# Two MoE layers on one core: groups 2 and 3 between the layers in a new order, and the last pages' results summed by TensorE

## What is computed

```
x = x + xattn0(ctx, layernorm(x))                 # 8 heads, masked
x = x + ffn0(layernorm(x))                        # top 2 of 8 experts (704 wide), silu(g)*u, and a shared one
h = rmsnorm(layernorm(x)) @ W_in.T + b_in
x = x + depool(rmsnorm(ctx)) + h                  # a scan over patches, one patch for many tokens
z = layernorm(x)
scores = sigmoid(z @ gate_w.T)                    # 32 experts in 8 groups
top 6 of the best 4 groups, weights normalised, * 2.5
x = x + sum over the 6 of weight * (relu(z @ up_w[e].T)**2 @ down_w[e].T)
      + relu(z @ shared_up.T)**2 @ shared_down.T
```

## Time and profile before

| | us |
|---|---|
| median of 3 runs | 887.16 (883.94 to 887.17) |
| the profiled execution | 888.47 |
| its span, first to last instruction | 886.6 |
| PE busy | 722.6 (82%) |
| DVE busy | 416.7 (47%) |
| ACT busy | 273.0 (31%) |
| POOL busy | 308.5 (35%) |
| layer 1's shared units and the steps of groups 2 and 3 | about 558 to 665 |
| layer 1's routed experts | about 670 to 859 |
| last results read back and summed | 859 to 887 |

### The profile page before, as it was taken

The page is one execution under the profiler, slowest core; times in us unless marked ns, Lnnn a source line. Parts: engine busy times, 40 slices in busy tenths (PEclk is TensorE's granted clock), DMA queues, the critical chain, the costliest instruction groups (busy, mean ns, idle before and its releaser), DMA issues.

```text
span 886.6 us, 14153 instructions
## 1 busy us (share of the span) xinstructions
PE 722.6 (82%) x4526; PEld 631.4 (71%) x4526; DVE 416.7 (47%) x1615; ACT 273.0 (31%) x620; POOL 308.5 (35%) x322
## 2 busy tenths in 40 slices
PE   3868886389999999999899888866776868787865
PEld 2647776289999999999899877533456757676754
DVE  4998664022333243546644742725104444456563
ACT  2636631022111111222223122321123455445540
POOL 1333307600010111100552354172712656556560
PEclk9898859589999999999999998796978899989998
DMA  8999992231776767755866624242646556587866
GB/s 257 396 296 268 257 252 97 102 125 53 231 231 219 218 221 244 246 169 190 304 218 232 217 89 170 92 166 87 217 154 189 177 158 191 164 288 243 285 215 250
DMA packets 93534, 181.22 MB, mean 204 GB/s; under 512 B 9857, under 2 KB 54998, under 8 KB 93182
## 3 DMA queue, kind: packets, MB, share of 16 engines
q1 hardware_dynamic: 78048, 138.67, 50.9%
q0 software_dynamic: 13344, 38.68, 11.6%
q10 hardware_dynamic: 2046, 2.71, 1.0%
HBM read 134.07 MB, written 65.62 MB: 225 GB/s over the span
## 4 chain that ended last, share of the span: by engine, by line
PE 56%; DVE 16%; issue 10%; another core or an unknown queue 6%; DMA 4%; ACT 3%; POOL 3%; SPq 1%; DVEq 0%; POOLq 0%; ACTq 0%
PE PB L618 16%; PE PB L655 11%; PE PB L632 5%; PE PB L825 4%; PE PB L816 4%; PE PB L763 3%; POOL rows_out L1930 3%; PE PB L777 2%; PE PB L804 2%; DMA X<-in_x 2%; PE PB L684 1%; PE PB L600 1%; DMA MEM<-rows_out 1%; DVE WK L1256 1%
## 5 line engine op out<-in xcount | busy, mean ns | idle before, releaser
L618 PE MATMUL PB<-XT,MEM 128*128 128x128 f32 x1584 | 185.9, 276 | 1.1 <-issue 1.1
L618 PEld LDWEIGHTS PB<-XT,MEM 128*128 128x128 f32 x1584 | 181.7, 193 | 1.5 <-issue 1.3
L1882 POOL DMA_INDIRECT sorted_y<-WK x36 | 34.5, 958 | 279.0 <-DVE WK L1470 279.0
L1891 POOL DMA_INDIRECT rows_in<-MEM x96 | 93.5, 974 | 65.1 <-DVE MEM L1674 36.6
L655 PE MATMUL PB<-MEM,WK 128*128 x432 | 99.7, 380 | 3.3 <-DVE MEM L1646 1.9
L825 PE MATMUL PB<-MEM,WK 128*128 x228 | 67.6, 424 | 32.0 <-DVE WK L1823 26.1
L655 PEld LDWEIGHTS PB<-MEM,WK 128*128 128x128 f32 x432 | 79.3, 190 | 13.2 <-issue 3.9
L1930 POOL DMA_INDIRECT rows_out<-WS,MEM x58 | 56.7, 977 | 64.4 <-ACT WS L1045 49.2
L825 PEld LDWEIGHTS PB<-MEM,WK 128*128 128x128 f32 x228 | 42.2, 207 | 41.2 <-issue 36.9
L1930 POOL DMA_INDIRECT rows_out<-MEM x56 | 56.2, 1003 | 40.5 <-ACT MEM L1045 25.7
L939 ACT ACTIVATE XT<-PB 128x256 f32<-128x256 f32 x52 | 19.8, 381 | 162.2 <-PE PB L600 134.2
(11 more groups left out here) (280 smaller groups left out, 1255.4 us busy)
## 6 DMA issues: line engine op xcount, KB each, us to landing
MEM<-in_w SPq DMA_DIRECT2D x36, 896.0 KB
rows_in<-in_consts SPq DMA_DIRECT2D x32, 600.0 KB, 12.2
MEM<-in_w SPq DMA_DIRECT2D x36, 512.0 KB
MEM<-rows_in SPq DMA_DIRECT2D x58, 300.0 KB
MEM<-rows_out SPq DMA_DIRECT2D x16, 768.0 KB, 7.0
MEM<-in_w SPq DMA_DIRECT2D x32, 256.0 KB, 2.8
MEM<-in_w SPq DMA_DIRECT2D x2, 3072.0 KB, 18.9
sorted_x<-MEM SPq DMA_DIRECT2D x1, 5070.0 KB, 39.7
```

The lines of the kernel that those rows point to most:

```text
L618: t = e.matmul(o[:, to:to + P], UPW[m][i % (3 - m)][:, k, c * P:(c + 1) * P], XT[:, n % 2, k, :], start=(k == 0), stop=(k == 1))
L1882: e.indirect_dma_start(out=DY, out_offset=bass.IndirectOffsetOnAxis(ap=DEST[:, i:i + 1], axis=0), in_=YS[:, i % 2, :], in_offset=None).the ...
L1891: e.indirect_dma_start(out=DX1, out_offset=bass.IndirectOffsetOnAxis(ap=SLOT1[:, i, j:j + 1], axis=0), in_=XR[:, i, :], in_offset=None).th ...
```

## The change

**A. The order between the layers.** "t1" of group 2 moves into the middle of the up product of block 34 (`SOON`), "wi" into the same block, "t2" to block 35; "ro" of group 2 now stands before the two late shared tiles' up products. "rank" is split: PE's part and `shares` stand before the last `down`, `slots` right behind it and ahead of group 3's "sum". Group 3's "q1" and "q2" are shared by ACT (two tiles) and DVE (two). Units 0 to 3 stand before group 3's "q1", "ro" of group 3 behind unit 5's `up1`. An item ("u", n), ("d", n) or ("drain", n) is `up1`, `down1` or DVE's add alone.

```diff
+STEP_AT2 = 0, 1, 1, 2, 3, 4
+SOON = {(SUM_AT[2] + 1, 1)}
...
-        ("turn", 1), ("down", -1), ("wi", 2), ("up", 0), ("q2", 2), ("up", 1), ("t2", 2), ("down", 0), ("ro", 2), ("down", 1),
+        ("turn", 1), ("down", -1), ("t2", 2), ("ro", 2), ("up", 0), ("up", 1), ("down", 0), ("rank", 2), ("shares", 2),
```

```diff
+OWN = (TOPK * GB[3] + E1) // 2
...
+def up_bank(s):
+    return 4 + s % (4 if s < OWN - 2 else 2)
...
+            def to_tokens(s, n_pairs):
+                q.wait_ge("by", s)
+                q.wait_ge("hot", s)
+                q.wait_ge("bh", OWN - 3)
+                for b in (2 * s, 2 * s + 1):
+                    last = b == 2 * n_pairs - 1
+                    for i in range(4):
+                        t = e.matmul(PB[:, 6 + i // 2, i % 2 * D:(i % 2 + 1) * D], HOT[b % 4][:, i * P:(i + 1) * P], YO[b % 4],
+                                     start=(b == 2 * OWN and i % 2 == 0), stop=last, skip_group_check=True)
...
+                if OWN <= s - 2 < n_pairs:
+                    to_tokens(s - 2, n_pairs)
...
-                for i in range(8, NT, 2):
-                    o = PB[:, i // 2, 0:D]
...
+            def one_hot(s):
+                for b in (2 * s, 2 * s + 1):
+                    t = e.tensor_scalar(HOT[b % 4], TOKENS, PT6[:, s // 2 % 2, b % 4:b % 4 + 1], None, ALU.is_equal)
...
+                        e.tensor_tensor(X[:, i - 1:i + 1, :], X[:, i - 1:i + 1, :],
+                                        PB[:, 6 + h, :].rearrange("p (t d) -> p t d", t=2), ALU.add).then_inc(
...
+                if 0 <= s - 2 < OWN:
...
+            for i in range(8, NT, 2):
+                y = Y6[place(i)]
+                q.wait_ge(f"l6_{place(i)}", i)
+                e.tensor_tensor(y[:, 0:3 * D], y[:, 0:3 * D], y[:, 3 * D:6 * D], ALU.add).then_inc(*q.mark("set1"))
+                for k in (1, 2):
+                    e.tensor_tensor(y[:, 0:D], y[:, 0:D], y[:, k * D:(k + 1) * D], ALU.add).then_inc(*q.mark("set1"))
+                e.tensor_tensor(X[:, i, :], X[:, i, :], y[:, 0:D], ALU.add).then_inc(*q.mark("sp", i))
...
+                if i in (6, 8, 10, 12):
+                    lo = TRASH + (GB[3] + i // 2 - 3) * P * TOPK
+                    e.dma_start(DY1[lo:lo + P * TOPK, :].rearrange("(p n) d -> p n d", p=P),
+                                ZERO[:, 0:D].unsqueeze(1).broadcast_to([P, TOPK, D])).then_inc(*q.land("zeroed1", i))
...
             def fetch6(i):
+                upto = min(TOPK * GB[GROUP[i] + 1] + E1, 2 * OWN) - 1
...
+            store(6)
+            for i in range(8, NT):
+                fetch6(i)
```

```diff
+ENDS = {s: s - 2 for s in range(2, NPR + 2)}
+ENDS[1] = ENDS.pop(2)
```

More of the change, by code:

```diff
@@ L961, in mid @@
                         q.wait_ge("t1", g - 1, 1)
-                    for i in range(4):
+                    for i in range(4 if g < 3 else 2):
                         t = e.activation(to[:, i, :], X[:, a + i, :], ACT.Identity, bias=R2[:, a + i:a + i + 1],
@@ L1065, in end1 @@
                     step(s, n_pairs)
[L1066 to L1070 removed]
+                for h in range(2):
+                    i = GB[3] + 2 * h
+                    q.wait_ge("total", h)
                     e.dma_start(od[:, i:i + 2, :], X[:, i:i + 2, :]).then_inc(*q.land("out_b", i))
```

218 lines of the change are left out of this document (136 added, 82 removed).

## The result

| | before | changed |
|---|---|---|
| median of 4 runs, us | 887.16 (883.94 to 896.89) | 899.65 (897.6 to 900.65) |
| ratio, 95% interval | | 1.0144 (1.0104 to 1.0184) |
| profiled execution, its span | 888.47, 886.6 | 900.34, 898.5 |
| first page's fetch | 666.89 | 673.87 |
| from there to the end | 219.7 | 224.6 |

What follows compares the result with a forecast made beforehand. It took PE to bound layer 0's blocks, POOL's row bursts to hold PE between the layers, and DMA latency and POOL the end. 888.5 - 12 - 5 = 871.5 profiled, so 870 us; range 850 to 884.

Steps and rivals of the forecast that it cites:

- Step (2): Between the layers: group 2's `shares` and `slots` end at 559.3, so its row burst starts 12.4 us sooner.
- step (1): Between the layers: group 2's picks no longer cost the path, so PE's unit 0 starts 3 to 4 us sooner.
- Step (4): Between the layers: the burst ends 12.4 us sooner, so the first hold ends at about 593, if PE's group 3 work precedes it.
- R2: Rival: between the layers PE is held as long, ro of group 3 after the hold; middle -2, 880 us, 16%.
- Step (3): Between the layers: group 3's sums come 6 us later on DVE, covered by units; priced at nothing, up to 4 us otherwise.
- Step (5): Between the layers: 11.7 us from sigmoid to first row DMA, so the second burst starts at 605 instead of 617.5.
- Step (6): Between the layers: what follows the second hold, four to five units, stays the same.
- The reading of the holds: Between the layers: from some 11 to 15 us into a POOL burst, handovers with PE arrive only when it is over.
- B, the end: Kernel's end: chains of DMA, PE and POOL all give 881 to 882 against 886.6, so -5 us.
- R4: Rival: at the end PE's added products run at its lower clock; +20 there, 895 us, slower, 6%.
- R3: Rival: the end gives nothing because POOL and DVE share ports; 875 us, 10%.
- The rule against B: Kernel's end: a shared-port lock would make POOL's and DVE's sums go in turn, giving 0 instead of -5.

Runs made afterwards that it cites:

- order_only: The kernel before with only the new order between the layers, the end as before: 902.38 us, 1.0072 of the kernel before.
- dve_sums: The changed kernel with POOL's four sums given to DVE, which sums all of tiles 8 to 15: 903.28 us, 1.0071 of the kernel before.
- end_only: The changed kernel with the new order between the layers taken back: 901.82 us, 1.0066 of the kernel before.
- late_memset: The kernel before with one small memset of POOL behind everything: 898.51 us in one execution.
- end_dve: The changed kernel with the old order, DVE summing tiles 8 to 15, and one store behind five fetches: 899.99 us, 1.0052 of the kernel before.
- no_burst2_c: The changed kernel without 23 of group 2's 24 row DMAs, zeros written instead, those rows missing: 885.76 us, 0.9878 of the kernel before.
- before_again: The kernel before, unchanged, profiled once more in a set without long waits: 773.64 us.
- after_again: The changed kernel as it is, run in a set without long waits: 777.86 us, 1.0015 of the kernel before.

## Why the prediction was wrong, point by point

**Step (2), group 2's places at 559.3.** They came at 566.4. `slots` take 5.1 us (561.30 to 566.37), but they stand behind the adds of both late shared tiles (557.47 and 560.97), and those wait for PE's `down`, which came later: DVE's `hidden` (L1503) was held until 556.94. That the row burst of group 1 held it follows from the theory of the bursts and was not tested there. The step took DVE's list as full and the shared results as done at 557.7, though the new order puts the picks ahead of their products. So step (1), unit 0 sooner by 3 to 4 us, became 3.3 later.

**Step (4) is the one that failed.** It said that the hold's end moves with the burst's end, to 593, provided that PE has done t1, wi, t2 and ro of group 3 before the hold. It had not. The burst moved 5.3 us ahead and "wi" 7.3 us back (571.41 before, 578.72 now), so "wi" fell 12 us into the burst instead of at its start, and two late signals that had lain elsewhere now stood one behind the other on the path, with t2 and ro after them. The sigmoid starts at 612.79 instead of 605.80: 7.0 us later, in these two traces the whole of the stage's loss (in the others it starts at 609.22 and 610.80 with the new order and at 603.38, 605.17 and 607.61 with the old). This is R2's place, "ro of group 3 comes after the hold", but R2 priced it at -2 and it cost +7, because the condition of step (4) was named and not checked: by its own numbers PE had to be done with ro by 559.5 + 15 = 574.5, where the kernel before does ro at 589.39 (PE's L704) and the new order puts more in front of it.

**Step (3), group 3's sums later on DVE, priced at nothing, or up to 4 us.** The sums now start at 566.28, behind the places, and q1, t1 and "wi" move back with them. That is how "wi" came into the hold: the price was sought in PE's cover and lay in the hold.

**Step (5), 11.7 us from the sigmoid to the burst,** held exactly: 612.79 to 624.50. Only its start was wrong. **Step (6)**, that what follows is the same, held between these two: from the burst's start to the first page's fetch it is 49.37 us in both (617.52 to 666.89, 624.50 to 673.87). That is partly luck. In the other traces with holes the stretch is 50.2 and 49.8 us with the new order (order_only, dve_sums) but 53.7, 52.5 and 52.5 with the old (end_only, late_memset, end_dve), so there the old order loses in the second burst some 3 us of what it had gained before it.

**The reading of the holds.** The profile of before could only suggest it, and no_burst2_c showed it. What was wrong in it is how a hold runs: it does not end once with the burst, but signals come in batches, the last some 4 us behind the burst. The trace of before has a batch in the middle already (ACT's timeline, then PE's):

```profile
593.08 0.60 ACT L1014 ACTIVATE WK<-PB 128x512 f32<-128x512 f32 x1 [4.96 <-PE PB L763]
...
584.25 3.27 PE L763 MATMUL PB<-MEM 128*128 128x512 f32 x4
```

This relu, the fifth of L1014 in the stage, is that of unit 4, whose `up1` PE ended at 587.52; it starts 5.6 us late, and 21 us into the burst, where the prediction let nothing through from 11 to 15 us on. The sign of "a hole that ends later than 3 us after the burst" came (600.56 against 596.87), and before has it too: its sigmoid starts at 605.80, 3.8 us behind its burst.

**B, the end, -5 forecast, +4.9 measured.** The step that failed is the join of the three chains, "the last of eight is there at 875.5. DVE's sum 2.34": it let one sum stand behind the fetches, while DVE has four to do and stands with all of them behind its last `one_hot`, and so behind PE. No sum of DVE waited for a DMA (its rows above have no bracket); the first began at 878.85, behind the last matrix. PE's chain was forecast to end at 877.9; 7.1 us that pair 51 came later with the middle (848.07 to 855.19) and 2.8 for the one pair at the lower clock make 887.8, and it ended at 887.96: R4's mechanism, met in one pair of five. POOL's chain was 15 us and took 19.1 (870.60 to 889.67), DVE's four tiles were 9.4 and took 16.7 with the two adds. DMA's chain would have begun at 854.6 + 7.1 = 861.7 and began at 866.07, because the working looked at what the fetches wait for and not at `store(6)` ahead of them in SP's list; by the reading of the trace these 4.4 us matter on the path only in how long POOL and DVE run side by side. R3, that the sharing gives the end nothing, was right in its mechanism, and short of the result by the wait for PE.

**The rule against B.** The trace of after has the duration: beside each other DVE's additions take 1.5 to 4.6 times as long as alone, POOL's of 768 columns take 1.80 with DVE idle and up to 2.52 beside it, where 1.51 was worked out, and the span of dve_sums, without POOL, is within 1 us of that of the kernel with it, from another set. The Trainium skill, "SBUF — State Buffer", section "SBUF: two separate sides", calls the shared ports an exclusive lock, by which one engine's additions wait for the other's; the trace agrees in that both engines lose time, but less than one whole instruction after the other would cost: a tile on each takes 5.1 us, where DVE alone needs 2.25 and POOL's first tile, mostly by itself, took 4.4 (870.60 to 875.00), 6.65 together. Against DVE alone, which does two tiles in 4.5 us, the help gains nothing. The prediction had set it aside on rows in which the two met rarely.

**Zeroing and 0/1 matrices at nothing.** The zeroing, right: 80.00 of 80 us. The matrices, costed at nothing for PE: it waited 2.86 us for them once, of which their own time is 0.9 (858.21 to 859.09); DVE could begin them only behind a multiplication (L1883) for which it had waited 3.49 us.

## What to carry to other kernels

Before moving a step to release a long burst of indirect DMAs sooner, write down which handovers between engines then fall into the burst: in runs with these long waits single handovers came up to 18 us late, each that depends on the one before paid for itself, and a burst that comes sooner can cost more than one that comes later. Measure before and after in the same set: here before alone moved by 1% between sets with the waits, and by 14 to 16% between sets with and without them. A transfer that no longer waits for data still waits for whatever is ahead of it in its queue, here a store. And additions given to POOL beside DVE's were paid by both engines' pace, and where nothing else ended as late also by the drain behind POOL's last one, so move them there only if DVE has other things to do.

## What the hardware showed that was not expected

- The same kernel took 887 to 897 us in some sets of runs and 776 in others. It lies in long waits, and not in the middle alone: from 125 to 242 us PE is busy for 92.27 of 117 us in no_burst2_c and for 115.65 in before_again. PE's granted clock over that stretch is 0.84 and 1.00. What decides between the two is open, and so is whether bursts make all of these waits.
- In a set with these waits, PE's signals reached DVE and ACT late, in batches 2.9 to 11.3 us apart, once POOL had issued indirect DMAs 1.27 us apart for some 10 to 20 us, and leaving one burst out removed the waits of its time. In the sets without, bursts of the same pace held nothing up.
- POOL's DRAIN took 9.42 us with an addition that took 0.79, and 1.5 us with a memset of 8 columns; in after_again the span ended only with it, 5 us after everything else.
